# Self attention of a decoder layer: two blocks' weighed sums together at odd blocks, projections and turns at even ones, and an earlier load of x

## The reference, cut to what matters

```
scores = einsum('bhqd,bhkd->bhqk', q, k) * scale + compute_bias(N, N, table)
out = einsum('bhqk,bhkd->bhqd', softmax(scores), v) @ w_proj.T + b_proj
x = _layernorm(x + self_attention(x))
x = _layernorm(x + cross_attention(x, ctx_1024, ctx_1024))
x = _layernorm(x + ffn(x))          # one of 8 experts for each row
```

## Time and profile before

| | |
|---|---|
| median of 3 runs | 1072.87 us (1067.04 to 1074.95) |
| profiled execution, own time | 1071.02 us |
| its span | 1069.2 us |
| PE busy | 942.3 us (88%) |
| ACT busy | 772.8 us (72%) |
| DVE busy | 675.9 us (63%) |
| POOL busy | 347.9 us (33%) |
| granted clock of PE, mean of the span | 0.937 of 2.4 GHz |

### The profile page before, as it was taken

The page is one execution under the profiler, slowest core; times in us unless marked ns, Lnnn a source line. Parts: engine busy times, 40 slices in busy tenths (PEclk is TensorE's granted clock), DMA queues, the critical chain, the costliest instruction groups (busy, mean ns, idle before and its releaser), DMA issues. The chain is left out here.

```text
span 1069.2 us, 17528 instructions
## 1 busy us (share of the span) xinstructions
PE 942.3 (88%) x5301; PEld 523.5 (49%) x5301; DVE 675.9 (63%) x1760; ACT 772.8 (72%) x1452; POOL 347.9 (33%) x340
## 2 busy tenths in 40 slices
PE   5599999999999999999999999962599889898891
PEld 2233444444444433333333333321599779888790
DVE  5276877777777777354546464753377667667672
ACT  1387777787877868899989898940478767686670
POOL 4043133140313111001112211221436666665664
PEclk9699999999999989999999999985699999898895
DMA  8988587978769576695587558400523334333441
GB/s 210 201 229 235 120 249 143 320 153 243 201 154 275 103 195 109 148 266 110 123 151 153 105 117 160 100 20 28 197 91 119 105 110 176 105 117 115 127 169 44
DMA packets 73546, 162.93 MB, mean 152 GB/s; under 512 B 16441, under 2 KB 40056, under 8 KB 63416
## 3 DMA queue, kind: packets, MB, share of 16 engines
q1 hardware_dynamic: 68088, 152.23, 56.5%
q0 software_dynamic: 5056, 9.20, 3.0%
q10 hardware_dynamic: 320, 0.52, 0.1%
HBM read 116.40 MB, written 49.54 MB: 155 GB/s over the span
## 5 line engine op out<-in xcount | busy, mean ns | idle before, releaser
L717 ACT ACTIVATE probs<-sc 128x512 f32<-128x512 f32 x1024 | 528.5, 607 | 110.6 <-DVE sc L799 82.7
L491 PE MATMUL sc<-qst,kst 57*128 57x512 f32 (+1 forms) x1024 | 269.5, 471 | 18.0 <-DMA qst<-s_qk 12.4
L799 DVE TENSOR_TENSOR sc<-sc,strip 128x308 f32<-128x308 f32 (+1 forms) x512 | 192.9, 429 | 101.7 <-PE sc L491 100.8
L503 PE MATMUL ot<-probs,vals 128*32 128x512 f32 x1600 | 215.0, 610 | 0.0
L491 PEld LDWEIGHTS sc<-qst,kst 57*128 57x128 f32 (+1 forms) x1024 | 118.1, 186 | 193.0 <-ACT probs L717 147.9
L1753 POOL DMA_INDIRECT f_rows<-s_x,f_get_ids x45 | 107.0, 2378 | 36.4 <-issue 34.8
L1611 ACT ACTIVATE f_h<-f_h_ps,f_par 128x384 f32<-128x384 f32 x104 | 64.0, 616 | 27.0 <-PE f_h_ps L1530 26.9
L1691 DVE TENSOR_TENSOR f_h_lo<-f_h,f_h_hi 128x384 fp32r<-128x384 f32 x104 | 56.9, 547 | 27.8 <-ACT f_h_hi L1612 27.4
L1189 POOL TENSOR_SCALAR veps<-mv_self 128x4 f32<-128x4 f32 x8 | 1.9, 232 | 192.3 <-DVE mv_self L857 192.3
L1612 ACT ACTIVATE f_h_hi<-f_h_ps,f_par 128x384 fp32r<-128x384 f32 x104 | 64.3, 618 | 0.0
L1252 POOL DMA_INDIRECT s_tokens<-ids,place_i x32 | 32.9, 1029 | 88.9 <-DVE place_i L943 81.6
(11 more groups left out here) (173 smaller groups left out, 1672.8 us busy)
## 6 DMA issues: line engine op xcount, KB each, us to landing
s_qk<-w_hi SPq DMA_DIRECT2D x32, 512.0 KB, 7.1
strip<-in_w_all SPq DMA_DIRECT2D x16, 1024.0 KB, 11.8
f_raw<-in_w_all SPq DMA_DIRECT2D x14, 1024.0 KB
kst<-s_qk SPq DMA_DIRECT2D x32, 256.0 KB, 6.1
qst<-s_qk SPq DMA_DIRECT2D x32, 256.0 KB, 7.4
s_x_parts<-split SPq DMA_DIRECT2D x16, 512.0 KB, 8.6
kst<-s_ctx_parts SPq DMA_DIRECT2D x32, 256.0 KB, 6.1
qst<-s_x_parts SPq DMA_DIRECT2D x32, 256.0 KB, 7.3
```

The source lines that it names most:

```text
L491: nc.tensor.matmul(sc[j][:], kst[at:at + rows, i, P * c:P * c + P], qst[at:at + rows, i, :], start=True, stop=True).then_inc(scored, 1)
L503: last = nc.tensor.matmul(sums_bank(n, g)[32 * j:32 * j + 32, :], vals[:, c, 4 * g + j, :], probs[:, k % KEPT, j, :], start=(c == 0), stop ...
L717: nc.scalar.activation(probs[:, k % KEPT, j, :], sc[j][:], ACT.Exp, scale=scale).then_inc(exped, 1)
L799: nc.vector.tensor_tensor(sc[j][:, lo:hi], sc[j][:, lo:hi], band_backwards(rank_of(4 * g + j), at, hi - lo), ALU.add).then_inc(biased, 1)
```

## The change

In batches 1 to 5 the load of `xT` for batch b + 2 stands at the beginning of the batch on SP, behind the load of `xnat` and ahead of the stores of the projections; batch 0 keeps its place. On PE, a self batch weighs nothing in an even block; in an odd block k it weighs blocks k - 3 and k - 2 behind its scores. `project_qk` stands in blocks 0 (two), 2 and 4, `project_v` in blocks 10 and 12 (two each), `project_out` in blocks 6 and 8 (two each), and both `turn_x1` in block 14. ACT, DVE and POOL keep their lists.

```diff
+            def load_xT(b):
+                sp.dma_start(xT[:], io["xT"][b].rearrange("(c p) n -> p c n", p=P)).then_inc(ld_xT, 16)
...
                 if b > 0:
                     sp.wait_ge(xb_ready, b)
                     sp.dma_start(xnat[:], io["x"][b].rearrange("(c p) n -> p c n", p=P)).then_inc(ld_xnat, 16)
+                if 0 < b < B - 2:
+                    sp.wait_ge(x_lo_ready, b)
+                    load_xT(b + 2)
                 if b < B - 1:
                     store_parts(b + 1, 0)
...
-                if b < B - 2:
-                    if b == 0:
-                        sp.wait_ge(v_mm, 4)
-                    else:
-                        sp.wait_ge(x_lo_ready, b)
-                    sp.dma_start(xT[:], io["xT"][b + 2].rearrange("(c p) n -> p c n", p=P)).then_inc(ld_xT, 16)
+                if b == 0:
+                    sp.wait_ge(v_mm, 4)
+                    load_xT(2)
...
-            def weigh_behind(n, k):
-                if k >= BEHIND:
-                    weigh(n, k - BEHIND)
+            def weigh_behind(n, k, behind=BEHIND):
+                if k >= behind:
+                    weigh(n, k - behind)
                 elif n > 0:
-                    weigh(n - 1, BLOCKS + k - BEHIND)
+                    weigh(n - 1, BLOCKS + k - behind)
...
             def end_self(b, k):
-                if 5 <= k < 9:
+                if k in (6, 8):
+                    project_out(b, k - 6)
                     project_out(b, k - 5)
-                if k in (14, 15):
-                    turn_x1(b, 15 - k)
+                if k == 14:
+                    turn_x1(b, 1)
+                    turn_x1(b, 0)
...
             def prepare_self(b, k):
-                if k < 4:
-                    project_qk(b, k)
-                if 9 <= k < 13:
-                    project_v(b, (k - 9) // 2, (k - 9) % 2)
+                if k == 0:
+                    project_qk(b, 0)
+                    project_qk(b, 1)
+                if k in (2, 4):
+                    project_qk(b, k // 2 + 1)
+                if k in (10, 12):
+                    for t in range(2):
+                        project_v(b, (k - 10) // 2, t)
...
                     scores(b, k)
-                    weigh_behind(b, k)
+                    if k % 2:
+                        weigh_behind(b, k, BEHIND + 1)
+                        weigh_behind(b, k)
```

## The result

The changed kernel took 1116.40 us (median of 4 runs, 1106.11 to 1121.72) against 1069.95 (median of 4, 1065.25 to 1074.95): ratio 1.042, 95% interval 1.033 to 1.052. It is 4% slower, where 1079 was forecast; the prediction is wrong.

A forecast was written before the change was run, and what follows sets the result against it. PE was taken as bound by some 42 us of work a batch plus 6 us of waits: boundary stalls and the scores-band-exponential chain. 1071.0 - 0.7 (batch terms) + 8.4 (clock) = 1078.7, said as 1079, range 1062 to 1094.

The forecast's parts named there:

- Part 1: Early load of x in batches 1 to 5: removes PE's stall in batches 2 to 6, 3.8 us gained, SP cost nothing.
- the chain: Scores, band, exponential, next scores: sets at least 5.43 us for a pair of blocks, in seven of eight pairs.
- Turning the sums: Four times a batch DVE waits for the pair's second weighed sum, delaying the next band: +1.1 us.
- the stall at block 0: PE idles at each batch boundary until the low half of x is ready; the early load removes it in batches 2 to 6.
- block 4's wait: Block 4's exponentials queue behind ACT's copy of the fourth projection, which PE now makes in block 4: +1.8 us.
- the places where the clock can fall: Block 4/5 of batches 1 to 6, three pairs in batch 0, five in batch 7: 14, half falling at 1.2, +8.4 us.
- Rival D: In the self batches PE's own work decides, not the chain: faster, 1055 us, 1050 to 1062; chance 0.10.
- Rival C: Clock falls at all 14 places, 1.2 to 1.9 us each: slower, 1087 to 1097 us; chance 0.24.
- Batches 0 and 1: Batch 0 +3.6 us from uncovered blocks and block 4's wait; batch 1 still waits for x and ends +3.5 in all.
- net zero in full batches: New order takes 47.1 us a batch against today's 47.0 to 47.1 without its stall, so reordering alone gains nothing.
- Part 2's saving: PE groups of one kind placed back to back save between 0 and 2.2 us of PE work a batch.
- The pair 8/9: Blocks 8 and 9 of a full batch, from block 8's scores to block 10's: 5.08 us forecast.

The follow-up runs named there:

- e2: The kernel before with the early load of x alone, in the old order: 1085.06 us, ratio 1.016.
- e3: The changed kernel with GpSimd's split of x held back until DVE's norm of x1 at block 13 is done: 1094.68 us, ratio 1.027.
- e4: The kernel before with the early load and GpSimd's split of x held back behind the norm: 1068.62 us, ratio 1.000.
- f3: e3 with GpSimd's split of the context held back until DVE's division of block 2 is done: 1084.16 us, ratio 1.013.
- f2: e3 with the fourth projection copied by ACT and subtracted by DVE in block 5 instead of block 4: 1079.08 us, ratio 1.009.
- f4: e3 plus one filler matmul, its result unused, in three even blocks of batch 0 and five of batch 7: 1084.54 us, ratio 1.013.

## Why the prediction was wrong

**Part 1 is the step that failed**: what POOL's split of x costs in its new place was put at nothing, without a reason. I followed each queue that the load was moved past on SP ("cost nothing", and no run speaks against that), and the split's place on POOL, and said when the split would run: "when block 12's value projection has been done, about 8 us before the batch ends". That was right, and I never asked what else runs in that window. It is DVE's norm of x1. e2 shows the cost by itself, 16 us lost in the old order instead of a gain of 3.8; e3 and e4 take most of it away without giving up the early load. The price has two terms: 2.1 us on DVE and thereby on the chain of bands, exponentials and scores, in five batches (10.6 in all by the long records), and then half clock behind PE's idle. Batch 6, the one without a split, was the control inside the changed kernel's own trace.

The trace of before had the sign, in batch 7, and I had not looked for it, since a mean over a line hides two records in 32:

```profile
382.82 1.84 DVE L815 TENSOR_TENSOR normed<-turned,rden 128x256 f32<-128x256 f32 x1
...
382.01 2.37 POOL L1208 TENSOR_TENSOR ctxT<-ctxT,ctx_hi 128x1024 fp32r<-128x1024 f32 x1
```

A division of 0.41 took 1.84 and ended just behind POOL's, at 384.66 and 384.38. From that row the bound of Part 1 would have been 0 to 2.4 a batch, the whole of POOL's record.

**"Turning the sums", +1.1, lacks a term.** The later weighed sum moves block 2's division too, into POOL's split of the context. A division was long nine times after the change, eight of them beside that split (10.2 us too much in all), and twice before (3.0 us). f3 prices it at 0.91 for a full batch and 10.5 in all, with batch 7's long division and three falls of the clock in block 5 gone too. It is 0.9 of the 1.1 missing at pair 4/5 of batch 5.

**Right**: the stall at block 0 (gone), the lengths of most pairs by the chain (table), block 4's wait (+1.8 forecast, 1.88 by f2), and the places where the clock can fall. Rival D, that PE's own work decides, is refuted: no pair of batches 2 to 6 was shorter than the chain's forecast by more than 0.13. Its own sum does not come out either: five batches at 2.97 and three at half of that are 19 us, not 16.

**The clock was mis-sized.** I had 14 places, half of them falling, 1.2 each, 8.4 in all. Twelve fell. In batch 7 all five did, at 2.0 each, above my upper end of 1.9; in block 5 of batches 1 to 6 five of six, 6.9 us; in batch 0 two of three, the pairs 6/7 and 8/9 at 7.27 and 6.93 against 5.75 and 5.42 in f4. Together that is some 20 us. The step to blame is reading the price from a place where one group of weighed sums stood behind the fall, and then going below the doubled figure; with pairs behind, all of the pair is at half clock and so are the next scores. Rival C, every place at 1.2 to 1.9, 17 to 27 us, was close on the clock, and its end of 1097 was low by the collisions, which it didn't hold.

**Batches 0 and 1** were forecast to end 3.5 late, with batch 1 waiting for x as before. They ended 9.9 late, and batch 1 has no idle ahead of its first projection: batch 0, with 56.25, was long enough for x to be there.

**Did the reorder net zero in full batches?** By the 47.1 forecast yes; in e3 they take 48.75. That is 1.35 above e4's 47.40. With the copy in block 5 and the division clear of POOL it is 46.35: the order is then worth 1.05 a batch at most, for e4 still holds its long division, and no run has the old order with that division clear of POOL. Part 2's saving was smaller than the waits that it brought.

**Open**: that POOL and DVE contend for a port is argued from lengths and ends of records, not shown; what is shown is that the long records vanish when the two operations are moved apart. What decides whether the clock falls in block 5 is not shown either: e3 has the same idle of 1.17 and the same scores spread over 1.96 or 1.97 in all of batches 1 to 6, and fell in three of them. The pair 8/9 stayed 0.5 above its forecast in every full batch, and the 6 us behind the self batches are not explained.

## What to carry to other kernels

When an operation moves on an engine that has time to spare, list what the other engines run in its new window, above all SBUF-to-SBUF work on DVE beside GpSimd; and look at maxima of a line's durations, not at its mean. After the move look again: in e4 the wait that freed the norm put the split beside a division. Where a reorder puts two groups behind one wait, move every copy that follows the moved producer with it, and keep the old order where there is no work left to lie in the gaps. A half of a rebalancing tried alone says nothing about the whole.

## What the runs showed of the hardware

**GpSimd's work lengthens DVE's, by where the operands lie.** DVE's norm (SBUF to SBUF) took 2.54 instead of 0.41 beside POOL's 2.38, its division 1.33 or 1.84 instead of 0.41, and these three ended 0.15 to 0.28 us behind POOL's end. In the self batches of all 13 profiles every norm or division of over 0.5 us, 93 of them, overlaps a record of POOL, and of the 599 that overlap none not one is that long. In the changed kernel POOL's subtractions for the low halves took 2.36 to 2.39, beside a long record or not. Bands and turns, which read PSUM, kept their lengths beside the same POOL instructions (a band of 308 columns 0.47 and 0.48, a turn 0.72 in e3 either way). The Trainium skill has this in SBUF — State Buffer, "Who interferes with whom": a DVE instruction with two SBUF inputs contends with a GpSimd instruction that reads SBUF, so does one in a two-port mode, which a tensor_scalar can enter, and in the latter case whoever issues first holds the shared ports for its whole instruction. The traces agree in which records are long and in the order of ends. They do not settle who came first at the norm: in the records DVE's begins 0.01 to 0.02 us ahead of POOL's, and yet it is DVE's that is long. The kernel-wide price, 16 us by e2, is this case's.

**An idle under 2 us can bring the clock down, and filler holds it.** Behind an idle of 1.58 and a group of scores spread over 2.26 the granted clock read 0.50, the 1.2 GHz level; with a matmul of 1.12 us in the gap it stayed at 1.00 for the whole batch, 2.0 us a place. The Trainium skill describes a clock that goes back and forth over such small gaps between groups on rotating PSUM banks in TensorE: Matmul & The Clock Gate, "A second HAM failure mode: psum-queue depth-cycling"; batch 7 agrees, 0.73 against 1.00 with the filler. An idle of 1.17 behind a projection and ahead of block 5's spread scores was followed by a fall in five of batches 1 to 6 of the changed kernel and in three of e3's; in the others the pair behind it took 1.92, at full clock.
